# First stage of a blur and group-norm kernel: small VectorE operations with one PSUM operand, and GpSimd's power written straight into a table

## What is computed

```python
def _gn(v, G=32, eps=1e-5):
    g = v.reshape(B_, G, C_ // G, H_, W_)
    m = jnp.mean(g, axis=(2, 3, 4), keepdims=True)
    s = jnp.var(g, axis=(2, 3, 4), keepdims=True)
    return ((g - m) / jnp.sqrt(s + eps)).reshape(v.shape)

# layer 0: a 4x4 blur (outer product of 1,3,3,1) of every channel
x = x + blur(_gn(x), kernel)
# layer 1: two 1x1 convolutions and a dynamic 3x3 filter on _gn(x), described below
x = x + layer_1(_gn(x), w_v, w1, gamma, beta, w2, b2)
```

## Time and profile before

| | |
|---|---|
| median of 3 runs | 5373.69 us (5371.09 to 5374.22) |
| the profiled execution | 5375.6 us, of which the trace's span is 5373.8 us |
| busy share of the span | PE 86%, DVE 93%, ACT 44%, POOL 84% |
| first stage | 0 to about 1219 us of the span |
| second stage | 1219 us to the end |
| mean granted clock of PE | 0.954 of 2.4 GHz |

### The profile page before, as it was taken

How to read it: one execution, slowest core, us unless ns; L and a number is a source line. 1 busy time by engine, 2 the same in 40 slices (tenths; PEclk the granted TensorE clock), 3 DMA queues, 4 the chain that set the end, 5 groups by cost and what they waited for, 6 DMA issues and landing times.

```text
span 5373.8 us, 140190 instructions
## 1 busy us (share of the span) xinstructions
PE 4631.7 (86%) x52820; PEld 2166.1 (40%) x52820; DVE 4995.1 (93%) x7994; ACT 2347.1 (44%) x3633; POOL 4513.0 (84%) x2208
## 2 busy tenths in 40 slices
PE   7888888887989898989888898989898989888874
PEld 2333333333434343434444443434343434444432
DVE  8999999993899999999999999999999999999998
ACT  7888888883333333332333232333333332333221
POOL 5777777771789998989899998989898989899999
PEclk9999999998999999999999999999999999999986
DMA  7888888873433333333323333323333333323221
GB/s 222 225 228 225 228 228 226 229 182 94 132 95 107 100 99 104 97 101 96 116 83 115 99 104 95 112 84 122 96 103 96 103 98 101 111 88 111 88 69 58
DMA packets 868592, 681.28 MB, mean 127 GB/s; under 512 B 555840, under 2 KB 818368, under 8 KB 851520
## 3 DMA queue, kind: packets, MB, share of 16 engines
q1 hardware_dynamic: 868032, 673.64, 42.2%
HBM read 405.08 MB, written 268.44 MB: 125 GB/s over the span
## 4 chain that ended last, share of the span: by engine, by line
PE 37%; DVE 18%; issue 11%; POOL 6%; ACT 4%; DVEq 1%; DMA 0%; ACTq 0%; POOLq 0%; SPq 0%
PE ps L666 18%; PE ps L650 13%; PE ps L680 7%; POOL acc L911 6%; DVE prod_p L962 5%; DVE ps L1003 3%; DVE ps L1006 2%; DVE ps L962 2%; DVE acc L1009 2%; DVE prod_d L962 2%; DVE six_t L927 1%; ACT xs L763 1%; ACT t L824 1%; ACT val L811 1%; DVE dev_t L943 1%
## 5 line engine op out<-in xcount | busy, mean ns | idle before, releaser
L911 POOL TENSOR_TENSOR acc<-acc,prod_p 128x1024 f32<-128x1024 f32 x1536 | 3652.4, 2378 | 386.6 <-DVE acc L1009 158.5
L666 PE MATMUL ps<-xm,wv 128*32 128x256 f32 (+1 forms) x32768 | 2113.7, 418 | 120.5 <-ACT val L811 90.3
L962 DVE TENSOR_TENSOR prod_p<-ps,val 128x1024 f32<-128x1024 f32 x1536 | 1855.2, 1214 | 67.3 <-POOL acc L911 65.9
L666 PEld LDWEIGHTS ps<-xm,wv 128*32 128x32 f32 x32768 | 1072.3, 112 | 1163.6 <-issue 556.5
L283 PE MATMUL ps<-xn,band 64*64 64x512 f32 x8192 | 956.6, 603 | 14.6 <-ACT x_out L243 6.4
L811 ACT ACTIVATE val<-ps 128x512 f32<-128x512 f32 (+1 forms) x640 | 345.7, 556 | 1326.0 <-PE ps L666 1035.6
L962 DVE TENSOR_TENSOR prod_d<-ps,val 128x512 f32<-128x512 f32 x1024 | 696.8, 680 | 148.5 <-ACT ps L817 145.0
L650 PE MATMUL ps<-xm,w 128*128 128x512 f32 x1536 | 696.4, 608 | 85.0 <-ACT val L811 65.5
L680 PE MATMUL ps<-t,w 128*32 128x256 f32 x9216 | 573.1, 406 | 227.0 <-ACT t L824 118.2
L243 ACT ACTIVATE x_out<-ps 64x512 f32<-64x512 f32 x1024 | 606.1, 592 | 183.4 <-PE ps L283 164.5
L315 POOL TENSOR_TENSOR x_out<-x_out,x_in 128x512 f32<-128x512 f32 x512 | 634.2, 1271 | 0.0
(11 more groups left out here) (59 smaller groups left out, 2723.6 us busy)
## 6 DMA issues: line engine op xcount, KB each, us to landing
x_in<-x SPq DMA_DIRECT2D x128, 1024.0 KB, 7.9
x<-x_out SPq DMA_DIRECT2D x256, 512.0 KB, 5.1
acc<-x SPq DMA_DIRECT2D x1024, 128.0 KB, 2.7
out<-acc SPq DMA_DIRECT2D x256, 512.0 KB, 2.7
xm<-x SPq DMA_DIRECT2D x192, 512.0 KB, 5.9
xs<-x SPq DMA_DIRECT2D x64, 512.0 KB, 6.4
wv<-wvt SPq DMA_DIRECT2D x1, 1024.0 KB, 7.9
w<-w1t SPq DMA_DIRECT2D x1, 512.0 KB, 8.3
```

Of the source, the lines that this page charges most:

```text
L666: mm = nc.tensor.matmul(ps[32 * q:32 * q + 32, b, at:at + ROWS[u] * W], wv[:, kt, (m + x) * 32:(m + x + 1) * 32], xm[:, kt, r0:r0 + ROWS[u ...
L911: nc.gpsimd.tensor_tensor(acc[:, r, :], acc[:, r, :], prod_p[:, k % P_RING, :], ALU.add).then_inc(p_added, 1)
L962: return nc.vector.tensor_tensor(dst.rearrange("p (m r w) -> p m r w", m=count, w=W), taps_of(tap).rearrange("p (m r w) -> p m r w", m=1, ...
```

## The change

The two SBUF operands of the second and third operation of `spreads` become one: the difference is computed twice, once into `dev` in SBUF and once into PSUM bank 7 (`dev_ps`); the square reads one of each and writes PSUM; the sum with the variance reads the square from PSUM. POOL writes `rstd` to a place of its own for each step, in a table with one row per image and step that all readers index, so line 387's copy into `table_s` is gone; ACT's scale operand and DVE's operand of `offsets` are now at an address that depends on the image. The last multiplications with `member` read the table by strides and are a plain `tensor_tensor`.

```diff
--- before.py
+++ after.py
@@ -118,7 +118,7 @@
     ones = sb("ones", [P, P])
     member = sb("member", [P, 2 * CG])
     power = sb("power", [P, 2 * GPS])
-    table_s = sb("table_s", [P, B, STEPS * GPS])
+    rstd = sb("rstd", [P, B + 1, STEPS, 2 * GPS])
     table_b = sb("table_b", [P, B, STEPS * GPS])
     pick = sb("pick", [P, B * KT, 2 * CG])
 
@@ -127,7 +127,6 @@
     dev = sb("dev", [P, 2 * GPS])
     spread = sb("spread", [P, 2 * GPS])
     var_eps = sb("var_eps", [P, 2 * GPS])
-    rstd = sb("rstd", [P, 2, 2 * GPS])
     norm_b = sb("norm_b", [P, 2, GPS])
 
     const_in = sem("a_const_in")
@@ -152,6 +151,7 @@
     picked = sem("picked")
 
     MEAN_BANKS, VAR_BANK = (4, 6), 5
+    DEV_BANK = 7
 
 
     NORM_LAG, BLUR_LAG, ADD_LAG, X1_LAG = 2, 3, 4, 5
@@ -227,9 +227,10 @@
                 act.wait_ge(norm_ready, i * STEPS + k + 1)
                 if has(i, k, N_RING):
                     act.wait_ge(blurred, i * (STEPS * TWO) + TWO * (k - N_RING + 1))
+            img, s = where(i, k)
             nc.scalar.activation(group(xn[:, r, :], XP, W, 2, g), group(x_in[:, k % X_RING, :], W, W, 0, g),
                                  ACT.Identity, bias=norm_b[:, k % 2, g:g + 1],
-                                 scale=rstd[:, k % 2, g:g + 1]).then_inc(xn_ready, 1)
+                                 scale=rstd[:, img, s, g:g + 1]).then_inc(xn_ready, 1)
 
         def keep_blur(i, k, two):
             r = k % OUT_RING
@@ -326,7 +327,8 @@
                 pool.wait_ge(xn_ready, i * (STEPS * GPS) + GPS * (min(k - 2, NS) if isinstance(i, int) else k - 2))
             if k >= 1 and (has(i, k, 1) or has(i, k, X1_LAG + 1)):
                 c = columns(i, k - 1)
-                nc.gpsimd.tensor_tensor(rstd[:, (k - 1) % 2, c], var_eps[:, c], power[:, c], ALU.pow)\
+                img, s = where(i, k - 1)
+                nc.gpsimd.tensor_tensor(rstd[:, img, s, c], var_eps[:, c], power[:, c], ALU.pow)\
                     .then_inc(rstd_done, 1)
             if adds:
                 add_x(i, k - ADD_LAG, 2)
@@ -360,12 +362,14 @@
             c = columns(i, k)
             dve.wait_ge(local_done, i * STEPS + k + 1)
             dve.wait_ge(mean_done, i * STEPS + k + 1)
-            nc.vector.tensor_tensor(dev[:, c], mv[:, c, 0], ps[:, MEAN_BANKS[k % 2], c], ALU.subtract)\
-                .then_inc(stats_chain, 1)
+            mean = ps[:, MEAN_BANKS[k % 2], c]
+            dev_ps, square = ps[:, DEV_BANK, c], ps[:, DEV_BANK, 2 * GPS + c.start:2 * GPS + c.stop]
+            nc.vector.tensor_tensor(dev[:, c], mv[:, c, 0], mean, ALU.subtract)
+            nc.vector.tensor_tensor(dev_ps, mv[:, c, 0], mean, ALU.subtract).then_inc(stats_chain, 1)
             dve.wait_ge(stats_chain, chain_at(i, k, 2))
-            nc.vector.tensor_tensor(dev[:, c], dev[:, c], dev[:, c], ALU.mult).then_inc(stats_chain, 1)
+            nc.vector.tensor_tensor(square, dev_ps, dev[:, c], ALU.mult).then_inc(stats_chain, 1)
             dve.wait_ge(stats_chain, chain_at(i, k, 3))
-            nc.vector.tensor_tensor(spread[:, c], dev[:, c], mv[:, c, 1], ALU.add).then_inc(spread_done, 1)
+            nc.vector.tensor_tensor(spread[:, c], square, mv[:, c, 1], ALU.add).then_inc(spread_done, 1)
 
         def add_eps(i, k):
 
@@ -380,12 +384,12 @@
 
         def offsets(i, k):
             dve.wait_ge(rstd_done, i * STEPS + k + 1)
+            now, at = where(i, k)
             if has(i, k):
-                offset(ps[:, MEAN_BANKS[k % 2], 0:GPS], rstd[:, k % 2, 0:GPS], norm_b[:, k % 2, :], norm_ready)
+                offset(ps[:, MEAN_BANKS[k % 2], 0:GPS], rstd[:, now, at, 0:GPS], norm_b[:, k % 2, :], norm_ready)
             if has(i, k, X1_LAG):
                 img, s = where(i, k - X1_LAG)
-                nc.vector.tensor_copy(table_s[:, img, s * GPS:(s + 1) * GPS], rstd[:, k % 2, GPS:2 * GPS])
-                offset(ps[:, MEAN_BANKS[k % 2], GPS:2 * GPS], rstd[:, k % 2, GPS:2 * GPS],
+                offset(ps[:, MEAN_BANKS[k % 2], GPS:2 * GPS], rstd[:, now, at, GPS:2 * GPS],
                        table_b[:, img, s * GPS:(s + 1) * GPS], table_done)
 
         def slot(i, k):
@@ -428,10 +432,12 @@
 
         dve.wait_ge(table_done, NS)
         n = 0
-        for table, dst in ((table_s, x1_scale), (table_b, x1_bias)):
-            nc.vector.scalar_tensor_tensor(out=pick[:], in0=table[:].rearrange("p b (t e) -> p (b t) e", e=2 * CG),
-                                           scalar=1.0, in1=member[:].unsqueeze(1).to_broadcast([P, B * KT, 2 * CG]),
-                                           op0=ALU.mult, op1=ALU.mult)\
+        of_x1 = rstd[:].rearrange("p b s e -> p (b s) e")[:, X1_LAG:X1_LAG + NS, GPS:]
+        scales = of_x1.rearrange("p (n t) c -> p n t c", t=2)
+        offsets_x1 = table_b[:].rearrange("p b (n t c) -> p (b n) t c", t=2, c=CG)
+        chosen = member[:].rearrange("p (n t c) -> p n t c", n=1, t=2).to_broadcast([P, B * KT, 2, CG])
+        for table, dst in ((scales, x1_scale), (offsets_x1, x1_bias)):
+            nc.vector.tensor_tensor(pick[:].rearrange("p n (t c) -> p n t c", t=2), table, chosen, ALU.mult)\
                 .then_inc(picked, 1)
             n += 1
             dve.wait_ge(picked, n)
```

## The result

The changed kernel takes 5241.98 us (median of 4 runs, 5241.05 to 5244.41) against 5373.95 before: a ratio of 0.9756, 95% interval 0.9739 to 0.9773, 132 us less. The forecast was 5248, in a range of 5233 to 5305. The profiled execution took 5241.05 us, its span is 5239.3.

A forecast was written before the change was run, and what follows sets the result against it. First-stage DVE, held by POOL's additions, makes PE wait; then PE binds at 8.10 us a step. 5375.6 less 124.3 and 1.5 is 5249.8, runs' median 1.9 lower: 5248 us, 5233 to 5265 (0.78); 8 in 10: 5233 to 5305.

The forecast's parts named there:

- The holds: First stage, DVE: copy, square and sum each held by one POOL addition; with a PSUM operand, 0.15 us each.
- The term that carries the sum: First stage: PE's wait for DVE's last aggregate before the mean, 124.3 us in 123 means, would go.
- either half buys the same time: First stage: copy removal alone, or PSUM operands, brings DVE under PE's 8.10 us step; the gains do not add.
- The 7.98 us that I gave DVE's chain: First stage: DVE's step with only the copy gone, 9.22 less one addition of 1.24 us, under PE's 8.10.
- The margin on the tight path: First stage, spreads' sum on PE to next mean: DVE's aggregates end 0.38 us before PE's blur, so no wait.
- The sum: Whole kernel: profiled 5375.6 us less 124.3 for PE's wait and 1.5 at the first stage's end, 5249.8 us.
- the low end of the range: 5233 us: PE's clock, 0.99 over the first stage, returns to full for 12 us; products and rounding add a few.
- Addresses from registers: First stage: register-dependent addresses for ACT's 512 normalizations, two DVE products and POOL's power; taken to cost nothing.
- The rival in which ACT stalls at them: First stage: each normalization begins with a pause; at 0.45 us, 62 us lost, about 5435 us; chance 0.06.
- the upper bound: First stage, ACT: four register operations of 0.053 us, 0.21 us a step, giving 8.13 us and costing 4 us.
- The DMAs: Rival, first stage: DMAs bind at 242 GB/s, 8.67 us a step; 5298 to 5318 us; chance 0.12 for 5265 to 5330.

The follow-up runs named there:

- two single-part runs: Copy gone, square and sum put back to SBUF operands in the changed kernel: 5245.36 us; PSUM operands alone in the kernel before, copy kept: 5242.91 us.
- half-blur run: Changed kernel with PE doing two of the four taps of the blur, so the blur is incomplete: 5194.68 us.
- the short additions: Kernel before with POOL's additions on half of their columns, nothing else changed: 5240.87 us.
- both stages: Changed kernel with one PSUM operand also given to the second stage's square of the spreads and last two affine steps: 5182.09 us.

## Why the prediction was right

**The holds.** Shown. The three operations end with GpSimd's additions, get short when the additions do, and the two that got a PSUM operand take 0.17 us with it; I had taken 0.15. The added subtraction costs no more than its 0.16.

**What it wins.** The term that carries the sum, PE's 124.3 us before the mean, went to 0.1. That either half buys the same time was argued from one addition less, and the two single-part runs show it: 5245 and 5243 us, to 5242 for both. The 7.98 us that I gave DVE's chain for the copy alone was too long, since the square got shorter as well, but it lay on the right side of PE's step.

**The margin on the tight path.** I gave 0.38 us between the aggregates' end and the mean; the timeline leaves 0.17. From the start of the spreads' sum DVE takes 3.79 us to the end of the aggregates where I had counted 3.64; the difference is starts and gaps between instructions. PE comes to the mean 0.06 us sooner. The mean is not delayed by it.

**Where the other 6 us come from.** The stage's 132.1 us can be set out from PE's groups before and after: the wait for the mean, 124.3 to 0.1, gives 124.2; PE is busy for 1029.57 and not 1043.14 us with the same matmuls, 13.6; its wait for the last spreads, 5.3 to 4.1, gives 1.2; and idle time of its own before the blur goes the other way, 14.6 to 21.5, costing 6.9. The sum had the first and the third of these (there 1.5).

The 13.6 us is for the larger part PE's clock, which in the forecast was the low end of the range, 12 us, and not in the sum. The blur's matmuls alone, before and after, take 8.4 us less for the same 8192 records:

```profile
L283 PE MATMUL ps<-xn,band 64*64 64x512 f32 x8192 | 956.6, 603 | 14.6 <-ACT x_out L243 6.4 <-issue 1.4
```

```profile
L284 PE MATMUL ps<-xn,band 64*64 64x512 f32 x8192 | 948.2, 598 | 21.5 <-issue 13.9 <-ACT x_out L244 1.6
```

Before, the granted clock fell to 0.50, that is 1.2 GHz, in five stretches of the steady part, about 17 us together by windows of 1 us, of which half is lost. This window lies in one of them:

```profile
515.00:516.00 1.00, 1.00 (x12) 0.47 (x8) 1.00 (x3) 0.00 (x0) 0.30 (x1) 0.50 0.92 200
```

After, the clock over the steady part is 1.00. The other 5 us of the 13.6 are not clock: the busy times of PE's single groups fall by 8.7 us only, and the rest is overlap between their records. A mean that doesn't wait, for one, begins before the recorded end of the matmul ahead of it (515.62 against 511.99 + 3.70 = 515.69 in the timeline above).

The 6.9 us is the gap ahead of the first half of the blur, 0.17 us in that timeline and put down to PE's own issue; before, it was 0.06 (502.58 + 0.39 to a start at 503.03). I had not seen it behind the wait for the mean, and it is part of why the step is 8.14 us and not 8.10. So what the sum left out went both ways, and that it lies within 6 us is in part luck.

**Addresses from registers.** Taken at nothing, and ACT shows nothing. The normalizations' group, before and after, takes 389.4 and 389.5 us, with idle time of 6.6 and 6.7 us ahead of its 512 instructions, and the pair takes 1.52 us in the half-blur run too, where ACT binds. The rival in which ACT stalls at them is out. ACT's step, which I took for 7.92 us and 0.18 under PE's, was mis-sized: with 7.75 to 7.82 even the 0.21 us of the upper bound would have stayed under PE's.

**The DMAs.** I gave this rival 0.12, at 8.67 us a step from a row of 242 GB/s. The row was no limit: the changed kernel moves 257 GB/s at a share of 0.96 and the floor is 268. Taking the 8.15 us for which the DMAs were at work as a guide to their floor was likewise too careful; it is 7.8, near the 7.74 us of DMA work that the forecast read from a step. The estimate from the Trainium skill's "DMA: Bandwidth & Descriptors", section "Why small descriptors are slow (HBM only)", was 5.7 us; no run here comes near it. The truth lay between the two, 0.3 us under PE.

**What stays open.** Why PE's clock fell to half in the kernel before, for some 3 us at a time in five places, and not in the steady part after, was not tried by itself. Each of the five kernels in which PE's wait for the mean is gone (the changed one, the two halves, the short additions and both stages) runs at a granted clock of 1.00 there, and the half-blur kernel, in which PE idles a third of the time, at 0.93; that PE's pauses are the cause is an inference from these.

## What to carry to other kernels

A tiny operation that takes a microsecond may be held by another engine: set its end beside the ends of what the other engines do in the timeline, and look for the same operation with other operands nearby. Then ask what the hold costs, which is not its own length but what the next engine waits for on its account: in one stage here 3 us of holds were worth 1 us a step and either of two remedies won it all, in the other nearly every microsecond counted. Before speeding up an engine further, cut the one that binds in an experiment and see how near the next ones are.

## What the runs showed that I had not expected

A held operation can get by: with additions of 0.7 us the unchanged copy fell from 1169 to 187 ns, and with another start time alone the unchanged square fell from 1061 to 338; a sum of the second stage, which starts in a gap between two additions, was never held. The largest surprise was the second stage, where 48 operations of two elements per partition cost 60 us of the kernel.
